# Second layer's attention: Pi spread by turns, its sums by one product with ones, the share moved from Wout to the weighted rows

## The chip, the cores and the metric

The kernel runs on one core of one Trainium2 chip. The metric is the device time of one execution in microseconds (us). Three runs of the kernel before gave 338.89, 339.13 and 342.37 us; the median is 339.13 us. Engines: PE is TensorE, DVE is VectorE, ACT is ScalarE, POOL is GpSimd, SP issues most DMAs. Each has its own instruction stream; they meet only through semaphores.

## The reference, cut to what matters

Two layers act on x of shape (16, 256, 128); each adds attention times silu(feed-forward) to x. The first layer is a softmax attention beside a mixture of experts; the change leaves it alone. The attention of the second layer (16 heads of 8 numbers, one softmax over the heads for each row):

```python
w = (x @ Wqkv.T).reshape(b, n, h, d).transpose(0, 2, 1, 3)
w_normed = w / jnp.maximum(norm, EPS_NORM)
logits = jnp.sum(w_normed * w_normed, axis=-1) * temp[None, :, :]
Pi = jax.nn.softmax(logits, axis=1)
Pi_norm = Pi / (jnp.sum(Pi, axis=-1, keepdims=True) + EPS_PI)
dots = jnp.einsum('bhn,bhnd->bhd', Pi_norm, w * w)
attn = 1.0 / (1.0 + dots)
out = -(w * Pi[..., None]) * attn[:, :, None, :]
return out.reshape(b, n, dim) @ Wout.T + bout
```

`attn` is one number for each column of a batch element. It can be put on the weighted rows or on Wout's rows. The feed-forward of the second layer picks one of 8 experts for each batch element, from its last row, and loads that expert's weights: they can be fetched only once the choice is known.

## The kernel before, in words

Everything stays in SBUF as 32 tiles of 128 rows. A batch element b is two tiles, a chunk c is two batch elements (b = 2c and 2c+1), so there are 16 elements and 8 chunks. All sums are kept transposed in the second layer: the 128 partitions are the columns of w (16 heads of 8), the free axis is the row n.

For a chunk the second layer goes: `norm1` (DVE, layer norm), `turn1` (PE, four transposes, copied out by ACT), `proj` (PE, w), `squares` (ACT, w squared with its norm) and `keep` (ACT, w itself into FT), `weigh` (DVE, the weights of the heads), `heads` (PE, logits, 16 columns), `center` (DVE), `soft` (ACT), `share` (DVE: Pi), `expand` (ACT: each of the 16 shares copied 8 times along the free axis, so that a tile of 128 rows holds 128 numbers each). Then for each b:

- `spread(b, k)` (PE, L664 to L671): two f32 products of the expanded Pi with identity and a column of ones (129 columns) into bank PS[k]. The first 128 columns are Pi turned, the last one its sum over the rows.
- `dots(b, k)` (DVE, L1316 to L1321): one custom instruction multiplies and adds up Pi times w squared (L1319, with an accumulator read behind it); one reduction adds the two sums (L1321).
- `attn_out(b, k)` (DVE, L1323 to L1326): w times Pi, into FT. It is the last reader of bank k and raises `s_ot`.

For a chunk `attention(c)` (DVE, L1328 to L1338) is three small dependent steps that give the share ATT, `weigh_out(c)` (ACT, L1757) makes two copies of Wout scaled by it, and `out1(c, k)` (PE, L673) multiplies the rows of FT by them. `end(c, k)` (DVE, L1344) adds the result to x, and SP stores it.

The feed-forward shares the engines: `ff_up` (L690), `ff_down` (L698), `ff_out` (L713) on PE, with gelu and bias on ACT and the residual on DVE (L1342). `choose1`, `choose2` (PE), `sel_logits`, `select` (DVE) choose the experts of eight elements at once (g = 0, 1); `select(1)` releases SP's loads of the experts 8 to 15 (L285 to L287).

The order of work on each engine is written out by hand: one list of calls for each engine. The eight PSUM banks are handed out by hand too. The third argument on PE names the semaphore to wait for before a bank is overwritten: `out1(1, 5, s_ot, 5)` waits until five `attn_out` are done, that is `attn_out(4, 5)`, and `heads(5, 2, s_ot, 7)` until `attn_out(6, 2)` is. Work behind such a wait on PE waits too.

Of the kernel before, what the change touches and what calls it, by code (L numbers as in the profile page):

```python
# [11 lines left out]
ALU = mybir.AluOpType  # L12
# [62 lines left out]
def program(nc, D, out):  # L75
    with ExitStack() as ctx:
# [3 lines left out]
        def sem(name):  # L80
# [71 lines left out]
        WOB = EP[:, 1, :].rearrange("p (b d) -> p b d", d=128)  # L152
# [33 lines left out]
        s_selx, s_soft, s_px, s_wob, s_h1, s_rt, s_g1 = (sem(n) for n in (  # L186
            "sel_exp", "soft", "pi_spread", "wout_weighted", "h1", "reasoned", "end_silu"))
# [138 lines left out]
        def _(e):  # L326
# [337 lines left out]
            def spread(b, k, free=None, n=0):  # L664
# [4 lines left out]
                for i in range(2):  # L669
                    m = e.matmul(PS[k][:, i * 129:(i + 1) * 129], PXP[c % 2][:, h, i * 128:(i + 1) * 128], C[:, 0:129], start=True, stop=True)  # L670
                m.then_inc(p_sp, 1)  # L671

            def out1(c, k, free=None, n=0):  # L673
                e.wait_ge(s_wob, c + 1)
# [5 lines left out]
                for i in range(4):  # L680
                    m = e.matmul(PS[k][:, i * 128:(i + 1) * 128], tile(WT, 4 * c + i), WOB[:, (2 * c + i // 2) % 8, :],
                                 start=False, stop=i == 3)
# [224 lines left out]
        def _(e):  # L907
# [405 lines left out]
            def pi(k):  # L1313
                return PS[k][:, 0:258].rearrange("p (i n) -> p i n", i=2)

            def dots(b, k):  # L1316
                e.wait_ge(p_sp, b + 1)
                w2 = w2v(b).rearrange("p (i n) -> p i n", i=2)
                e.tensor_tensor_reduce(w2, pi(k)[:, :, 0:128], w2, 1.0, 0.0, ALU.mult, ALU.add,  # L1319
                                       DOT[:, b:b + 1]).then_inc(s_vec, v.up())  # L1320
                e.tensor_reduce(SPI[:, b:b + 1], pi(k)[:, :, 128], AX, ALU.add).then_inc(s_vec, v.up())  # L1321

            def attn_out(b, k):  # L1323
                w = tile(WT, 2 * b, 2).rearrange("p (i n) -> p i n", i=2)
                e.wait_ge(s_w, b // 2 + 1)
                e.tensor_tensor(w, pi(k)[:, :, 0:128], w, ALU.mult).then_inc(s_ot, 1)  # L1326

            def attention(c):  # L1328
# [9 lines left out]
                                       op1=ALU.mult).then_inc(s_attn, 1)  # L1338

# [100 lines left out]
            attn_out(0, 6)  # L1440
            weigh(2)
            dots(1, 0)
            center(2, 4)
# [4 lines left out]
            attention(0)  # L1448
            attn_out(2, 5)
            dots(3, 2)  # L1450
            sel_logits(0, 7)
            attn_out(3, 2)
            attention(1)
# [14 lines left out]
            attn_out(4, 5)  # L1468
# [17 lines left out]
            attention(3)  # L1486
# [9 lines left out]
            dots(9, 3)  # L1496
            attn_out(8, 7)
# [4 lines left out]
            dots(11, 7)  # L1502
# [570 lines left out]
```

## Time and profile before

| | before |
|---|---|
| median of three runs | 339.13 us |
| lowest, highest run | 338.89, 342.37 us |
| span of the profiled execution (first to last instruction) | 338.1 us |
| granted TensorE clock, mean over the span | 0.995 of full |
| PE busy | 312.5 us (92%) |
| DVE busy | 208.9 us (62%) |
| ACT busy | 206.7 us (61%) |
| POOL busy | 138.5 us (41%) |

The profiled execution's own device time is not listed beside its span. The shortest run, 338.89 us, is 0.8 us above the span, the median 1.0 us. The second layer's attention, the part that changes, lies between 249 us (the first `spread`) and the end. The chain of waits names, for each moment, the work that the end of the program hung on. The timeline lists instructions of one engine by start; where an engine sat idle before, the row tells how long and what released it. A busy engine's rows overlap a little, so the cost of a step is best read as the distance between the starts of neighbours.

### The profile page before, as it was taken

The page shows a single profiled execution, that of the slowest core. Times are in us where ns is not written, and L with a number is a line of the kernel's source. Part 1 is how long each engine was busy: PE and PEld are TensorE (multiplying, and loading weights), DVE is VectorE, ACT ScalarE, POOL GpSimd, SP SyncE. Part 2 cuts the span into 40 slices and gives each one's busy share as a digit, 9 for nine tenths or more (in the row PEclk, how much of TensorE's full clock was granted, in tenths as well). Part 3 has the DMA queues.
Part 4 walks back from the last instruction along what each step waited for, and adds up shares of the span by engine and source line. Part 5 has one row for each costly group of instructions (what it writes and reads, how often), then busy time and mean ns, then how long its engine had stood idle before and what let it go on. Part 6 is the DMA issues. An engine that isn't in the chain of part 4 may idle for free.

```text
span 338.1 us, 7770 instructions
## 1 busy us (share of the span) xinstructions
PE 312.5 (92%) x2077; PEld 259.6 (77%) x2077; DVE 208.9 (62%) x779; ACT 206.7 (61%) x504; POOL 138.5 (41%) x152
## 2 busy tenths in 40 slices
PE   7879999999999799999998899898879999989994
PEld 6657555669999799999988767688854588768793
DVE  4999792225776765556544457665365848578465
ACT  2296754348776666565654435674586768897772
POOL 2200577777777746666664434454540000000000
PEclk9999999999999999999999999999997999999999
DMA  6980023113431113333333721111006532017403
GB/s 187 294 367 4 32 66 104 56 49 87 105 95 57 48 33 89 94 92 87 103 94 108 261 65 35 55 33 33 31 7 244 120 77 57 3 32 211 133 17 109
DMA packets 29321, 31.91 MB, mean 94 GB/s; under 512 B 7120, under 2 KB 22610, under 8 KB 29152
## 3 DMA queue, kind: packets, MB, share of 16 engines
q1 hardware_dynamic: 24960, 22.97, 24.1%
q0 software_dynamic: 4320, 8.47, 7.5%
q8 instruction: 18, 0.29, 0.4%
q14 instruction: 23, 0.19, 0.2%
HBM read 19.86 MB, written 12.01 MB: 94 GB/s over the span
## 4 chain that ended last, share of the span: by engine, by line
PE 72%; DVE 11%; ACT 5%; issue 5%; SPq 2%; DMA 2%; DVEq 1%; ACTq 0%
PE PS L474 19%; PE PS L486 9%; PE PS L414 4%; PE PS L690 3%; PE PS L401 3%; PE PS L440 3%; PE PS L698 3%; PE PS L626 2%; PE PS L390 2%; PE PS L392 2%; PE PS L627 2%; PE PS L642 2%; PE PS L628 2%; DVE XA L924 2%; PE PS L454 2%
## 5 line engine op out<-in xcount | busy, mean ns | idle before, releaser
L2010 POOL DMA_INDIRECT yc_scratch<-YS,XS x71 | 71.6, 1009 | 61.1 <-ACT YS L1609 44.6
L474 PE MATMUL PS<-XG,XT 128*128 128x128 f32 x568 | 76.7, 278 | 6.9 <-issue 3.0
L474 PEld LDWEIGHTS PS<-XG,XT 128*128 128x128 f32 x568 | 69.0, 192 | 10.1 <-issue 6.3
L1126 DVE COPY XT<-WE 128x512 f32 x71 | 30.9, 435 | 38.5 <-issue 21.3
L1602 ACT ACTIVATE EP<-PS 128x256 f32<-128x256 f32 x71 | 27.0, 383 | 43.3 <-PE PS L474 42.3
L486 PE MATMUL PS<-WE,EP 128*128 x284 | 43.9, 278 | 1.9 <-ACT YS L1609 1.8
L2001 POOL DMA_INDIRECT xs_scratch<-XA,POS x32 | 31.4, 981 | 29.9 <-DVE POS L1035 20.5
L486 PEld LDWEIGHTS PS<-WE,EP 128*128 128x128 f32 x284 | 37.6, 191 | 5.9 <-issue 5.9
L1117 DVE TENSOR_TENSOR EP<-EP,PS 128x256 f32<-128x256 f32 x71 | 29.6, 417 | 18.4 <-PE PS L486 15.9
L2001 POOL DMA_INDIRECT xs_scratch<-XB,POS x32 | 31.2, 976 | 9.8 <-issue 9.8
L1609 ACT ACTIVATE YS<-PS,XS 128x128 f32<-128x128 f32 x71 | 26.0, 366 | 5.2 <-PE PS L486 2.0
L944 DVE TENSOR_TENSOR EP<-EP,PS 128x512 f32<-128x512 f32 x16 | 10.8, 684 | 17.4 <-PE PS L392 17.4
L924 DVE TENSOR_SCALAR XA<-X,MV,RS 128x128 f32<-128x128 f32 x64 | 18.8, 362 | 0.6
L1578 ACT ACTIVATE EP<-EP,NM 128x256 f32<-128x256 f32 x32 | 15.9, 500 | 4.0 <-PE PS L428 4.0
L440 PE MATMUL PS<-F,EP 128*128 128x128 f32 x128 | 16.3, 276 | 1.7 <-DVE EP L1109 1.7
L401 PEld LDWEIGHTS PS<-WB,EP 128*128 128x128 f32 x128 | 15.1, 192 | 3.3 <-DVE EP L944 2.3
L440 PEld LDWEIGHTS PS<-F,EP 128*128 128x128 f32 x128 | 15.5, 192 | 2.1 <-DVE EP L1109 1.9
L913 DVE BATCH_NORM_STATS2 ST<-X 128x6 f32<-128x128 f32 x64 | 13.7, 276 | 4.8 <-DMA X<-in_x 4.8
L1093 DVE CUSTOM_DVE_ANT_0 EP<-PS,C 128x256 f32<-128x256 f32 x32 | 12.3, 420 | 6.9 <-PE PS L414 4.2
L390 PE MATMUL PS<-XT,WB 128*128 128x512 f32 x32 | 16.5, 597 | 0.0
L401 PE MATMUL PS<-WB,EP 128*128 128x128 f32 x128 | 15.9, 277 | 0.6 <-DVE EP L944 0.6
L392 PE MATMUL PS<-XT,WB 128*128 128x512 f32 x32 | 16.3, 592 | 0.0
(190 smaller groups left out, 601.3 us busy)
## 6 DMA issues: line engine op xcount, KB each, us to landing
XS<-xs_scratch SPq DMA_DIRECT2D x71, 65.0 KB, 1.9
XB<-yc_scratch SPq DMA_DIRECT2D x16, 256.0 KB, 4.4
S<-in_w SPq DMA_DIRECT2D x13, 256.0 KB, 2.6
WE<-in_we SPq DMA_DIRECT2D x1, 3072.0 KB, 14.8
X<-in_x SPq DMA_DIRECT2D x16, 128.0 KB, 3.0
out<-X SPq DMA_DIRECT2D x16, 128.0 KB, 1.8
yc_scratch<-YS,XS POOLq DMA_INDIRECT x71, 2.3
SH<-in_w SPq DMA_DIRECT2D x3, 256.0 KB, 2.5
```

Of the source, the lines that this page charges most:

```text
L390: e.matmul(PS[k][:, :], WB[:, f * 128:(f + 1) * 128], tile(XT, 4 * c, 4), start=True, stop=True).then_inc(p_g, 1)
L401: m = e.matmul(PS[1][:, t * 128:(t + 1) * 128], HHS[:, (2 * c + f) % 3, t * 128:(t + 1) * 128], WB[:, 512 + f * 128:512 + (f + 1) * 128], ...
L440: m = e.matmul(PS[k][:, i * 128:(i + 1) * 128], PT[:, kb, j, i * 128:(i + 1) * 128], F[:, 2 * b + j, :], start=j == 0, stop=j == 1)
L474: m = e.matmul(PS[k][:, f * 128:(f + 1) * 128], WC[:, u % 4, f * 128:(f + 1) * 128], XG[:, g % 2, j * 128:(j + 1) * 128], start=True, stop ...
L486: m = e.matmul(PS[k][:, 0:128], HHE[:, u % 3, f * 128:(f + 1) * 128], WE[:, bass.ds(reg[u] + (512 + f * 128), 128)], start=f == 0, stop=f ...
L924: m = e.tensor_scalar(XA[:, t, 0:128], X[:, t, :], MV[:, t, 0:1], RS[:, t:t + 1], ALU.subtract, ALU.mult)
L1117: e.tensor_tensor(HHE[:, u % 3, :], SGE[:, u % 3, :], PS[u % 3 if u < BESIDE else u % 2][:, 256:512], ALU.mult).then_inc(s_hhe, 1)
L1126: e.tensor_copy(WC[:, u % 4, :], WE[:, bass.ds(r, 512)]).then_inc(s_wc, 1)
L1602: e.activation(SGE[:, u % 3, :], PS[u % 3 if u < BESIDE else u % 2][:, 0:256], ACT.Silu, bias=0.0, scale=1.0).then_inc(s_sge, 1)
L1609: e.activation(YS[:, u % 8, :], PS[(5, 7)[u % 2] if u < BESIDE else 5][:, 0:128], ACT.Copy, bias=0.0, scale=XS[:, g % 4, j, 129:130]).then ...
L2001: e.indirect_dma_start(out=xs, out_offset=bass.IndirectOffsetOnAxis(ap=POS[:, s, t:t + 1], axis=0), in_=T[:, t, :], in_offset=None, bounds ...
L2010: e.indirect_dma_start(out=yc, out_offset=bass.IndirectOffsetOnAxis(ap=XS[:, g % 4, j, 128:129].bitcast(U32), axis=0), in_=YS[:, u % 8, :] ...
```

## The change: Pi turned instead of multiplied, sums for a chunk at once, the share on the rows

1. `spread` transposes the expanded Pi (two transposes for each b). For the first element of a chunk it adds one product of ones (128x128) with the chunk's 64 columns of Pi: 64 sums, one for each tile and head, in every partition, in columns 256 to 319 of the same bank.
2. `sums(c, k)` on DVE takes each element's 32 columns, masks them with the head of the partition and adds them up: two custom instructions for a chunk, the second after a wait for the first (they share a scratch). The reduction in `dots` goes.
3. `attn_out` multiplies by Pi and by the share ATT in one instruction, and so waits for `attention(c)`. `weigh_out` on ACT goes with its buffer and semaphore, and `out1` multiplies by Wout itself as soon as both `attn_out` of its chunk are done.
4. The list of DVE is reordered: `dots(2c)`, `dots(2c+1)`, `attention(c)`, and only then the two `attn_out`. The list of PE has the same calls in the same order with the same bank guards.

```diff
 def spread(b, k, free=None, n=0):
                 for i in range(2):
-                    m = e.matmul(PS[k][:, i * 129:(i + 1) * 129], PXP[c % 2][:, h, i * 128:(i + 1) * 128], C[:, 0:129], start=True, stop=True)
+                    m = e.transpose(PS[k][:, i * 128:(i + 1) * 128], PXP[c % 2][:, h, i * 128:(i + 1) * 128], ident)
+                if h == 0:
+                    m = e.matmul(PS[k][:, 256:320], ONE[:, 0:128], LG[:, c, :, :].rearrange("p i h -> p (i h)"),
+                                 start=True, stop=True)
 def out1(c, k, free=None, n=0):
-                e.wait_ge(s_wob, c + 1)
+                e.wait_ge(s_ot, 2 * c + 2)
...
+            def sums(c, k):
+                sc = WA[:, 84:116].rearrange("p (i h) -> p i h", i=2)
+                for h in range(2):
+                    if h == 1:
+                        e.wait_ge(s_vec, v.n)
+                    e.tensor_tensor_reduce(sc, PS[k][:, 256 + 32 * h:288 + 32 * h].rearrange("p (i h) -> p i h", i=2),
+                                           c_("head").unsqueeze(1).broadcast_to([128, 2, 16]), 1.0, 0.0, ALU.mult, ALU.add,
+                                           SPI[:, 2 * c + h:2 * c + h + 1]).then_inc(s_vec, v.up())
 def dots(b, k):
-                e.tensor_reduce(SPI[:, b:b + 1], pi(k)[:, :, 128], AX, ALU.add).then_inc(s_vec, v.up())
+                if b % 2 == 0:
+                    sums(b // 2, k)
 def attn_out(b, k):
-                e.tensor_tensor(w, pi(k)[:, :, 0:128], w, ALU.mult).then_inc(s_ot, 1)
+                e.wait_ge(s_attn, b // 2 + 1)
+                e.scalar_tensor_tensor(out=w, in0=pi(k), scalar=ATT[:, b:b + 1], in1=w, op0=ALU.mult,
+                                       op1=ALU.mult).then_inc(s_ot, 1)
...
 # DVE's list, chunks 2 and 3
             dots(4, 5)
             norm1(4)
-            attn_out(4, 5)
             norm1(5)
             ff_out(1, 7)
             norm1(6)
             dots(5, 2)
+            attention(2)
+            attn_out(4, 5)
             norm1(7)
             weigh(4)
             attn_out(5, 2)
-            attention(2)
             center(4, 3)
             dots(6, 2)
             weigh(5)
+            dots(7, 6)
+            attention(3)
             attn_out(6, 2)
-            dots(7, 6)
             center(5, 2)
...
 # ACT: weigh_out(0) to weigh_out(7) taken out of the list
```

**First place, DVE around `attn_out(4)`.** Before, from `dots(4)` (L1319) over `norm1(4)` to `attn_out(4)` (L1326, which frees bank 5):

```order
L1319 ISA F,SM<-PS5,F 128x256 [waits pe_spread]
L1319 ISA SM 128x1
L1321 TENSOR_REDUCE SM<-PS5 128x1
L921 RECIPROCAL RS<-RS 128x4 [waits deviation1]
L924 TENSOR_SCALAR XA<-X,MV,RS 128x128 [waits vector_steps]
L924 TENSOR_SCALAR XA<-X,MV,RS 128x128 x3
L1326 TENSOR_TENSOR FT<-PS5,FT 128x256 [waits w_kept]
```

Now the end of `norm1(5)`, then `ff_out(1)` (L1356), `norm1(6)`, `dots(5)` (L1333), `attention(2)` and `attn_out(4)` (L1351):

```order
L926 TENSOR_SCALAR XA<-X,MV,RS 128x128 x3
L1356 SCALAR_TENSOR_TENSOR F<-PS7,XA 128x512 [waits pe_ff_out]
L923 RECIPROCAL RS<-RS 128x4 [waits deviation1]
L926 TENSOR_SCALAR XA<-X,MV,RS 128x128 [waits vector_steps]
L926 TENSOR_SCALAR XA<-X,MV,RS 128x128 x3
L1333 ISA F,SM<-PS2,F 128x256 [waits pe_spread]
L1333 ISA SM 128x1
L1339 SCALAR_TENSOR_TENSOR SM<-SM 128x2 [waits vector_steps]
L1342 RECIPROCAL SM<-SM 128x2 [waits vector_steps]
L1344 SCALAR_TENSOR_TENSOR SM<-SM 128x2 [waits vector_steps]
L1351 SCALAR_TENSOR_TENSOR FT<-PS5,SM,FT 128x256 [waits attention,w_kept]
```

`attn_out(4)` has moved behind two layer norms, one `ff_out`, `dots(5)` and `attention(2)`. On PE the step that overwrites bank 5 (`out1(1)`, after `turn1(4)`) stands where it stood.

**Second place, DVE around `attn_out(6)`, which frees bank 2.** Before, from `dots(6)` to `dots(7)` (bank 6), with `weigh(5)` (L1271 to L1277) between:

```order
L1319 ISA F,SM<-PS2,F 128x256 [waits pe_spread]
L1319 ISA SM 128x1
L1321 TENSOR_REDUCE SM<-PS2 128x1
L1271 TENSOR_SCALAR SM<-SM 128x2 [waits norm2]
L1273 RECIPROCAL SM<-SM 128x2 [waits vector_steps]
L1277 TENSOR_TENSOR WB<-SM 128x32 [waits vector_steps]
L1326 TENSOR_TENSOR FT<-PS2,FT 128x256 [waits w_kept]
L1319 ISA F,SM<-PS6,F 128x256 [waits pe_spread]
```

Now, from the end of `sums(3)` on:

```order
L1324 ISA SM 128x1
L1333 ISA F,SM<-PS2,F 128x256
L1333 ISA SM 128x1
L1273 TENSOR_SCALAR SM<-SM 128x2 [waits norm2]
L1275 RECIPROCAL SM<-SM 128x2 [waits vector_steps]
L1279 TENSOR_TENSOR WB<-SM 128x32 [waits vector_steps]
L1333 ISA F,SM<-PS6,F 128x256 [waits pe_spread]
L1333 ISA SM 128x1
L1339 SCALAR_TENSOR_TENSOR SM<-SM 128x2 [waits vector_steps]
L1342 RECIPROCAL SM<-SM 128x2 [waits vector_steps]
```

`dots(7)` and `attention(3)` now stand before `attn_out(6)`, which is the next row but one.

**Third place, PE from `spread(6)` to `heads(5)`, the step that overwrites bank 2.** Before:

```order
L670 MATMUL PS2<-C,SH 128x129 [waits attn_out,pi_spread]
L670 MATMUL PS2<-C,SH 128x129
L634 MATMUL PS4<-C,XA 128x128 [waits xt1,xn]
L634 MATMUL PS4<-C,XA 128x128 x3
L642 MATMUL PS3<-XT,WD 128x512 [waits centered,xt1]
L670 MATMUL PS6<-C,SH 128x129 [waits w_kept,pi_spread]
L670 MATMUL PS6<-C,SH 128x129
L649 MATMUL PS2<-WB,F 128x16 [waits attn_out,head_weights]
```

Now:

```order
L669 MATMUL PS2<-C,SH 128x128 [waits attn_out,pi_spread]
L669 MATMUL PS2<-C,SH 128x128
L671 MATMUL PS2<-C,ONE 128x64
L633 MATMUL PS4<-C,XA 128x128 [waits xt1,xn]
L633 MATMUL PS4<-C,XA 128x128 x3
L641 MATMUL PS3<-XT,WD 128x512 [waits centered,xt1]
L669 MATMUL PS6<-C,SH 128x128 [waits w_kept,pi_spread]
L669 MATMUL PS6<-C,SH 128x128
L648 MATMUL PS2<-WB,F 128x16 [waits attn_out,head_weights]
```

Nothing moved here: `heads(5)` still follows `spread(7)` directly and still waits for `attn_out(6)`; only what it waits for has moved on DVE.

## Rows read from the trace of the kernel before

**Rows 1.** The page: the chain that ended last, share of the span by engine.
```profile
PE 72%; DVE 11%; ACT 5%; issue 5%; SPq 2%; DMA 2%; DVEq 1%; ACTq 0%
```
**Rows 2.** Chain of waits in order of time, 255 to 301 us: start us, us, what.
```profile
300.75 0.24 DVE SELI L1303 x2
```
**Rows 3.** Single lines of code: duration ns min/median/max, first and last start us.
```profile
L670 PE MATMUL PS<-C,EP x32: 273/275/356, 250.6 to 316.7; 128*128 128x129 f32 x32
...
L634 PE MATMUL PS<-C,XA x32: 272/273/332, 216.5 to 292.2; 128*128 128x128 f32 x32
...
L1762 ACT ACTIVATE EP<-WD,SM x16: 384/392/401, 257.1 to 327.9; 128x128 f32<-128x128 f32 x16
```
**Rows 4.** PE timeline, 282 to 305 us: start, us, what, idle before.
```profile
282.51 0.61 PE L713 MATMUL PS<-WD,WB 128*128 128x128 f32 x4
...
283.82 0.60 PE L634 MATMUL PS<-C,XA 128*128 128x128 f32 x4
284.26 0.38 PE L618 MATMUL PS<-BR,ROWS 128*128 128x512 bf16 x1
...
291.36 0.69 PE L670 MATMUL PS<-C,SH 128*128 128x129 f32 x4
...
293.19 0.61 PE L670 MATMUL PS<-C,SH 128*128 128x129 f32 x4
293.63 0.98 PE L649 MATMUL PS<-WB,F 128*128 128x16 f32 x8
294.46 0.37 PE L656 MATMUL PS<-XT,WD 128*128 128x8 f32 x2
...
304.76 1.13 PE L690 MATMUL PS<-XT,S 128*128 128x256 f32 x4 [1.67 <-DMA WA<-in_b]
```
**Rows 5.** DVE timeline, 279 to 286 us.
```profile
280.46 0.18 DVE L921 RECIPROCAL RS<-RS 128x4 f32<-128x4 f32 x1 [0.84 <-ACT RS L1534]
...
283.28 0.68 DVE L1342 SCALAR_TENSOR_TENSOR F<-PS,XA 128x512 f32<-128x512 f32 x1
283.88 0.16 DVE L921 RECIPROCAL RS<-RS 128x4 f32<-128x4 f32 x1
...
285.11 0.42 DVE L1319 CUSTOM_DVE_ANT_0 F<-PS,F 128x256 f32<-128x256 f32 x1
285.45 0.08 DVE L1319 DVE_READ_ACCUMULATOR2_ANT SM<- 128x1 f32 x1
```
**Rows 6.** DVE timeline, 289 to 294 us: `attention(2)`, then `dots(7)`.
```profile
289.24 0.15 DVE L1332 SCALAR_TENSOR_TENSOR SM<-SM 128x2 f32<-128x2 f32 x1
289.42 0.17 DVE L1335 RECIPROCAL SM<-SM 128x2 f32<-128x2 f32 x1
289.62 0.16 DVE L1337 SCALAR_TENSOR_TENSOR SM<-SM 128x2 f32<-128x2 f32 x1
...
293.83 0.42 DVE L1319 CUSTOM_DVE_ANT_0 F<-PS,F 128x256 f32<-128x256 f32 x1 [0.40 <-PE PS L670]
```
**Rows 7.** Groups of DVE work, 249 to 338 us: busy us, mean ns of one.
```profile
L1285 DVE TENSOR_TENSOR C<-PS,WA 128x64 f32<-128x64 f32 x6 | 1.3, 224 | 0.2
L1277 DVE TENSOR_TENSOR WB<-SM 128x32 f32<-128x32 f32 x6 | 1.1, 192 | 0.2
```
**Rows 8.** Stretches: length, busy PE, PEld, DVE, ACT, POOL, granted clock, DMA, GB/s.
```profile
246.90:249.60 2.70, 1.58 (x12) 1.35 (x12) 1.99 (x9) 2.67 (x6) 1.73 (x2) 1.00 0.05 9
...
256.00:259.40 3.40, 3.40 (x6) 1.44 (x6) 1.59 (x9) 2.39 (x5) 0.00 (x0) 0.50 0.95 347
...
301.00:304.70 3.70, 2.03 (x15) 1.65 (x15) 3.18 (x17) 3.08 (x7) 0.00 (x0) 1.00 0.42 82
```
**Rows 9.** Chain of waits: the same `add_up` steps on PE at either clock.
```profile
256.12 1.88 PE PS L626 x2
258.00 1.63 PE PS L627 x2
...
261.67 0.86 PE PS L627 x2
```

More of the change, by code:

```diff
@@ L1318, in dots @@
                 w2 = w2v(b).rearrange("p (i n) -> p i n", i=2)
[L1319 to L1326 removed]
+                if b % 2 == 0:
+                    sums(b // 2, k)
+                e.tensor_tensor_reduce(w2, pi(k), w2, 1.0, 0.0, ALU.mult, ALU.add, DOT[:, b:b + 1]).then_inc(s_vec, v.up())
             def attention(c):
@@ L1338, in attention, with attn_out @@
                                        op1=ALU.mult).then_inc(s_attn, 1)
+            def attn_out(b, k):
+                w = tile(WT, 2 * b, 2).rearrange("p (i n) -> p i n", i=2)
+                e.wait_ge(s_w, b // 2 + 1)
+                e.wait_ge(s_attn, b // 2 + 1)
+                e.scalar_tensor_tensor(out=w, in0=pi(k), scalar=ATT[:, b:b + 1], in1=w, op0=ALU.mult,
+                                       op1=ALU.mult).then_inc(s_ot, 1)
             def ff_out(c, k):
@@ L1439, in _ @@
             dots(0, 6)
-            attn_out(0, 6)
             weigh(2)
             dots(1, 0)
+            attention(0)
+            attn_out(0, 6)
             center(2, 4)
@@ L1447, in _ @@
             center(3, 6)
-            attention(0)
+            dots(3, 2)
+            attention(1)
             attn_out(2, 5)
-            dots(3, 2)
             sel_logits(0, 7)
             attn_out(3, 2)
-            attention(1)
             select(0)
@@ L1485, in _ @@
             attn_out(7, 6)
-            attention(3)
             center(6, 4)
@@ L1496, in _ @@
             dots(9, 3)
+            attention(4)
             attn_out(8, 7)
@@ L1502, in _ @@
             dots(11, 7)
+            attention(5)
             end(2, 4)
@@ L1509, in _ @@
             dots(12, 6)
-            attention(4)
             dots(13, 0)
+            attention(6)
             ff_out(4, 5)
             attn_out(12, 6)
-            attention(5)
             attn_out(13, 0)
-            attention(6)
             dots(14, 3)
+            dots(15, 1)
+            attention(7)
             attn_out(14, 3)
-            dots(15, 1)
             attn_out(15, 1)
             ff_out(5, 7)
-            attention(7)
             end(4, 2)
@@ L1755, in expand @@
                 m.then_inc(s_px, 1)
-            def weigh_out(c):
-                e.wait_ge(s_attn, c + 1)
-                if c >= 4:
-                    e.wait_ge(p_o1, c - 3)
-                for b in (2 * c, 2 * c + 1):
-                    m = e.activation(WOB[:, b % 8, :], d_("wout"), ACT.Copy, bias=0.0, scale=ATT[:, b:b + 1])
-                m.then_inc(s_wob, 1)
             def ff_up(b, k):
@@ L1889, in _ @@
             choose1(0, 1)
-            weigh_out(0)
             soft(2)
@@ L1893, in _ @@
             soft(3)
-            weigh_out(1)
             gated(4, 4)
@@ L1924, in _ @@
             squares(5, 6)
-            weigh_out(2)
             keep(5, 6)
@@ L1938, in _ @@
             keep(7, 2)
-            weigh_out(3)
             expand(5)
@@ L1967, in _ @@
             gate1(5)
-            weigh_out(7)
             ff_down(14, 0)
```

12 lines of the change are left out of this document (4 added, 8 removed).

## The prediction, written before the changed kernel ran

> **What bounds the kernel now.** I read the page's chain first: PE carries 72% of it, DVE 11%, DMA and SP's queue 2% each [rows 1]. So work taken off PE should count, and a wait put on PE should count in full, except where PE itself waits for somebody. The chain in order of time shows where it does in the changed part: from 256 to 295 us it is PE's own work almost without a break, then it turns to DVE (`center(6)` to `select(1)`, the choice of the second eight experts, done at 300.99 [rows 2]), to SP, and to the load of an expert's weights; PE stood still for 1.67 us and took up `ff_up(8)` at 304.76 [rows 4]. `select(1)` hangs on `choose1`, `choose2` and `heads(6)`, which stand on PE behind `heads(5)`. So whatever delays PE before 297 us delays the load and all that follows. The end of the program is PE-bound again, with a short tail on DVE and one store. The kernel is tight in this sense: a saving on PE is worth itself, and the guards of the banks decide whether there is a saving at all.
>
> **PE's work.** A f32 product leaves two records here: 16 `spread` of two products would be 64, half of them reading EP are 32 [rows 3]. A transposed tile leaves one: 8 `turn1` of four tiles are 32 [rows 3]. The distance from start to start is 0.44 us for four records of either kind: 283.82 to 284.26 for four transposes, 293.19 to 293.63 for the two products of `spread(7)` [rows 4]. So two transposes take 0.22 where two products took 0.44: minus 0.22 us for each of 16 elements, 3.5 us. The product with ones, two passes of 64 columns, is not in the trace. Its bounds are passes of 16 columns, 0.83 us for eight (293.63 to 294.46 [rows 4]), 0.10 each, and passes of 129 columns, 0.11 each; I take 0.21 for two. Eight of them add 1.7 us. The first `spread` of a chunk thus changes by 0.01, the second by 0.22. Where PE carries the chain that is: `spread(5)` at 270 us, `spread(11)` at 308 and `spread(15)` at 324; `spread(1)` and `(3)` lie before a wait of PE for DVE, `(9)` and `(13)` before waits for weights, and `(7)` is dealt with below.
>
> **ACT's work.** `weigh_out` goes, 16 instructions of 0.39 us, 6.3 us in all [rows 3]. ACT waits for PE or DVE before nearly every group in this part, so I cost the gain at nothing; nothing in the places below waits for ACT. `out1` needed the scaled Wout before and needs the two `attn_out` now; it stands so late in PE's list that neither is what it waits for, with one exception, next but one.
>
> **DVE's work.** Each chunk gets two masked sums over 32 columns. Their nearest rows are a tensor operation on 32 columns, 0.19 us, and one reading 64 columns of PSUM, 0.22 [rows 7], each with an accumulator read that costs about 0.01 beyond overlap (285.11 and 0.42 against 285.45 and 0.08 [rows 5]) and a wait of some 0.04 between them: 0.46 for the pair, with 0.40 and 0.60 as bounds. The reduction saved two times 0.07. `attn_out` with a scalar I cost like before, 0.42: on 512 columns the three-operand form took 0.68 (283.28 [rows 5]), less than twice 0.42. Eight chunks give 8 x (0.46 - 0.14), about 2.5 us more on DVE, which has idle time nearly everywhere. What counts is not this work but the order.
>
> **First new stall: `out1(1)` on PE waits for `attn_out(4)`.** Before, PE began it at 284.26 [rows 4], two us after DVE had freed bank 5. PE is 0.22 early by then (`spread(5)`), so it will ask at 284.04. DVE: `norm1(4)` waited 0.84 us for ACT's root and began at 280.46 [rows 5]; that idle time swallows the sums of chunk 2, and the root comes with PE, so it begins at 280.24. `norm1(4)` and `norm1(5)` take 1.23 each (the distance 283.88 to 285.11 [rows 5]), `attn_out(4)` no longer stands between them, and they end at 282.70. `ff_out(1)` waits for PE's product, 282.51 + 0.61 - 0.22 [rows 4], so it starts at 282.92, and takes 0.60 (283.28 to 283.88 [rows 5]). `norm1(6)` takes 1.23 again, to 284.75. `dots(5)` to the end of its accumulator read takes 0.42 (285.11 to 285.53 [rows 5]): 285.17. `attention(2)` starts 0.04 later and takes 0.54 (289.24 to 289.78 [rows 6]): 285.75. Another 0.04 for its own semaphore, then `attn_out(4)` 0.42: 286.21. With 0.04 to PE, `out1(1)` starts at 286.25. That is 1.99 us later than before, and 2.21 us of idle PE. Behind it stand `ff_down(5)`, `proj(4)` and everything up to the choice of experts, none of which had slack on PE: all moves by 1.99.
>
> **Second new stall: `heads(5)` waits for `attn_out(6)`.** `spread(7)` starts at 293.19 + 1.99 = 295.18. Its second transpose ends 0.11 + 0.27 later, 295.56, and `dots(7)` follows in 0.03 as before (293.19 + 0.61 to 293.83 [rows 4, 6]). DVE is there in time: `spread(6)` ends at 291.36 + 0.69 + 1.99 = 294.04 [rows 4], then `sums(3)` 0.46, `dots(6)` 0.42 and the three small steps of `weigh(5)`, 0.52 (like the first three of `attention`), come out at 295.5 with 0.1 to spare; this is the one place where dearer sums would show. Then 0.42 for `dots(7)`, 0.04 + 0.54 for `attention(3)`, 0.04 + 0.42 for `attn_out(6)`, 0.04 to PE: 295.59 + 1.50 = 297.09. Before, `heads(5)` began at 293.63 [rows 4]: it is 3.46 late, 1.47 more than the first stall left. `center(5)` to `select(1)`, SP and the load have nothing of their own that was waited for in parallel, so `ff_up(8)` starts at 304.76 + 3.46 = 308.22.
>
> **After that** the other moved `attn_out` are late by 0.7 to 1 us on DVE, but their banks are asked for later still: `spread(11)` wants `attn_out(8)` 4 us after it was done, `out1(3)` wants `attn_out(9)` 3 us after, the others 1.5 us or more. `end(2)` comes about 0.6 later against the rest and its store just keeps its turn in SP's queue before the load of expert 13; at most 0.3 could come of it. `spread(11)` and `spread(15)` give back 0.22 each.
>
> **Sum:** + 1.99 + 1.47 - 0.44, and 0.02 for the first `spread`s of later chunks: + 3.0 us on a span of 338.1, 341.1. The median of the runs stands 1.03 above that span, so the time is 339.13 + 3.0 = **342.2 us**, 0.9% slower. I call anything within 1%, 335.7 to 342.5 us, no change, since that is about what a measurement of this kernel can tell.
>
> **A rule against the change.** The clock fell once in the changed part: 0.50 (the 1.2 GHz level) from 256.0 to 259.4 [rows 8], and that cost (1.88 - 0.86) + (1.63 - 0.86) = 1.8 us [rows 9]. In 246.9 to 249.6, where 8 transposes were 1.04 of PE's 1.58 busy us, it stayed at 1.00 [rows 8]. The Trainium skill (TensorE: Matmul & The Clock Gate, Part 4: PE-mode transpose) says that transposes do not count as busy for the clock gate as products do. By that rule the clock would drop where transposes replace products next to idle time; the rows of this case neither bear it out nor exclude it.
>
> **Rivals.**
> - *The clock falls once more* (chance 0.22). Two new waits of 2.2 and 1.5 us, and shorter `spread`s around the wait for weights, leave PE less to do between 284 and 308 us. For: the fall at 256.0 shows that this part can lose the clock. Against: from 301 to 304.7 PE was busy only 2.03 of 3.7 us and kept it [rows 8]. Price as in [rows 9]: up to 1.8 us on the path, 342.2 + 1.8 = 344.0, or 343.3 if only part of it meets chained work.
> - *The guards don't bind and only the savings stay* (0.06): the other side. PE would gain 3 to 4 times 0.22, 338.3 us. It decides at one point: `attn_out(4)` done before 284.04 and `attn_out(6)` before 295.4. For it speaks that DVE is 62% busy; against it that the five steps in front of `attn_out(4)` all have their durations in the rows and 2.2 us would have to go.
> - *Only the first stall costs* (0.12): some of what follows `heads(5)` was late for a reason that I don't see, and swallows the second. 342.2 - 1.5 = 340.7 us.
> - *The turn isn't cheaper* (0.05): if a transpose fed by the expanded Pi needed two passes, nothing is saved on PE and each product with ones adds 0.21, six of them on the path: + 0.66 + 1.2, 344.0 us. The one record for each tile in [rows 3] speaks against it.
>
> The forecast keeps 0.55, with 341.6 to 342.9 as its own range (sums at 0.60 add 0.05 to 0.2, waits of DVE at 0.06 instead of 0.04 add 0.1, the store 0.3); about a third of it lies above 342.5. Slower by over 1%: 0.55/3 + 0.22 + 0.05 = 0.45; within 1%: 0.37 + 0.12 + 0.04 = 0.53; faster by over 1%: 0.02, part of the second rival. The range 340.5 to 344.2 leaves out the second rival, the upper edge of the first and half of the fourth.
>
> **What would show it.** `out1(1)` on PE with 2.2 us idle before it, released by DVE's `attn_out`; `heads(5)` with 1.5 us idle before it; two records for each `spread` and two more for each chunk; `weigh_out` gone from ACT with no new wait on ACT; `ff_up(8)` near 308.2. I am wrong if PE has no wait at `out1(1)`, if a step of `attention` with its waits takes more than 0.25, or if the clock's row shows a second fall.

## The result: 2.4% slower, outside the range

Beside runs of the kernel before on the same chip, the changed kernel took 349.5 us in the median of 4 runs (347.72 to 354.24), the kernel before 340.75 us (338.89 to 345.58). The ratio is 1.0236, with a 95% interval of 1.015 to 1.0322. Another 6 runs, in a later set, gave 350.42 against 340.86 us, 1.0237 [1.0186, 1.0288]. Every ratio here is taken over the executions that are not more than 1.5% above the fastest of their kernel, while the medians and means of times count all of them. The forecast was 342.2 us (340.5 to 344.2). So 8 to 10 us were lost (8.0 and 8.1 by the ratios, 8.8 and 9.6 by the medians) where 3.0 were forecast.

The profiled execution of the changed kernel was the longest of the four: 354.24 us, span 352.4 us, mean granted clock 0.944 (0.952 to 0.975 in the other three). What it shows of the clock's falls is therefore more than usual. The page has the chain by engine, which answers to [rows 1], and the clock in 40 slices of 8.8 us:

```profile
PE 79%; DVE 9%; issue 4%; ACT 3%; DMA 2%; SPq 1%; DVEq 1%; ACTq 0%
PEclk9678999999999999999999999999789998858998
```

PE's share of the chain grew from 72 to 79%, though the change took work off PE. The second row shows one reason: the clock is down in three places. Slices 2 to 4 lie in the first layer, which the change leaves alone; slices 29 and 30 hold a longer form of the fall that before had too [rows 8]; slices 34 to 37 are new. The last slice holds a fall from 350.2 us on, at the end of the program.

The PE timeline around the two places of the prediction, 289 to 336 us (start, us, what, idle before):

```profile
289.08 0.60 PE L633 MATMUL PS<-C,XA 128*128 128x128 f32 x4
292.01 0.42 PE L617 MATMUL PS<-BR,ROWS 128*128 128x512 bf16 x1 [2.34 <-DVE FT L1351]
292.23 1.92 PE L683 MATMUL PS<-WD,FT 128*128 128x128 f32 x8
...
302.53 0.38 PE L669 MATMUL PS<-C,SH 128*128 128x128 f32 x2
304.71 1.04 PE L648 MATMUL PS<-WB,F 128*128 128x16 f32 x8 [1.81 <-DVE FT L1351]
305.60 0.37 PE L655 MATMUL PS<-XT,WD 128*128 128x8 f32 x2
306.42 0.20 PE L661 MATMUL PS<-WD,A 128*8 128x8 f32 x2 [0.45 <-ACT A L1750]
306.54 2.08 PE L641 MATMUL PS<-XT,WD 128*128 128x512 f32 x2
...
318.11 1.81 PE L692 MATMUL PS<-XT,S 128*128 128x256 f32 x4
```

Both forecast stalls are there with the releaser forecast: `out1(1)` (the row at 292.01) waited 2.34 us for `attn_out`, `heads(5)` (304.71) 1.81 us. They answer to the rows of 284.26 and 293.63 in [rows 4], which had no wait. Behind each stands something that wasn't forecast: eight products of L683 took 1.92 us, where eight of the same kind took 1.05 later (323.20), and `proj` (L641) 2.08 where it took 1.02 at 299.10. And `ff_up(8)` (318.11) no longer waits for its weights at all, as it did in [rows 4]: PE itself had become later than the load. The stretches give the clock (columns as in [rows 8]):

```profile
249.00:258.00 9.00, 7.19 (x29) 5.34 (x29) 4.43 (x19) 6.24 (x15) 3.98 (x5) 0.63 0.04 10
292.00:295.40 3.40, 3.38 (x13) 3.10 (x14) 1.10 (x4) 0.00 (x0) 0.00 (x0) 0.53 0.00 0
306.60:320.00 13.40, 13.40 (x53) 11.35 (x53) 7.27 (x38) 9.17 (x24) 0.00 (x0) 0.52 0.19 46
```

The clock was at its lower level (0.50 of full, 1.2 GHz) for 3.4 us right behind the first stall (292.2 to 295.6) and for 13.6 us behind the second (305.9 to 319.5), of which PE was busy for all of the 3.4 and for 13.2 of the 13.6 us: it was the bound there. Behind the second stall come narrow products, `heads` of 16 columns and the choices of 8.

DVE before `out1(1)`, to be held against [rows 5] and [rows 6], and the pair of sums:

```profile
284.40 0.16 DVE L1324 CUSTOM_DVE_ANT_1 WA<-PS,C 128x32 f32<-128x32 f32 x1
284.49 0.08 DVE L1324 DVE_READ_ACCUMULATOR2_ANT SM<- 128x1 f32 x1
284.61 0.19 DVE L1324 CUSTOM_DVE_ANT_1 WA<-PS,C 128x32 f32<-128x32 f32 x1
284.72 0.08 DVE L1324 DVE_READ_ACCUMULATOR2_ANT SM<- 128x1 f32 x1
...
290.71 0.16 DVE L1339 SCALAR_TENSOR_TENSOR SM<-SM 128x2 f32<-128x2 f32 x1
290.91 0.17 DVE L1342 RECIPROCAL SM<-SM 128x2 f32<-128x2 f32 x1
291.11 0.16 DVE L1344 SCALAR_TENSOR_TENSOR SM<-SM 128x2 f32<-128x2 f32 x1
291.38 0.48 DVE L1351 SCALAR_TENSOR_TENSOR FT<-PS,SM,FT 128x256 f32<-128x256 f32 x1
```

### The profile page after: what moved, and what is told of

The parts are those of the page before. It is cut to its first block, busy times and chain, and to the rows that moved or that the text cites. A ratio compares the mean times of both kernels' runs of the same rounds, so it can differ in the third digit from the quotient of the medians.

```text
span 352.4 us, 7750 instructions
## 1 busy us (share of the span) xinstructions
PE 324.6 (92%) x2061; PEld 269.2 (76%) x2061; DVE 212.4 (60%) x795; ACT 202.8 (58%) x488; POOL 138.5 (39%) x152
## 4 chain that ended last, share of the span: by engine, by line
PE 79%; DVE 9%; issue 4%; ACT 3%; DMA 2%; SPq 1%; DVEq 1%; ACTq 0%
PE PS L473 18%; PE PS L485 9%; PE PS L692 4%; PE PS L413 4%; PE PS L700 4%; PE PS L439 4%; PE PS L400 4%; PE PS L389 3%; PE PS L391 3%; PE PS L641 2%; PE PS L715 2%; PE PS L347 2%; PE PS L625 2%; PE PS L683 2%; PE PS L627 2%
## 5 line engine op out<-in xcount | busy, mean ns | idle before, releaser
L485 PE MATMUL PS<-WE,EP 128*128 x284 | 45.0, 283 | 2.3 <-ACT YS L1623 1.8
L485 PEld LDWEIGHTS PS<-WE,EP 128*128 128x128 f32 x284 | 38.5, 195 | 6.4 <-issue 6.2
L400 PEld LDWEIGHTS PS<-WB,EP 128*128 128x128 f32 x128 | 16.4, 206 | 3.2 <-DVE EP L946 2.5
L389 PE MATMUL PS<-XT,WB 128*128 128x512 f32 x32 | 18.3, 656 | 0.0
L400 PE MATMUL PS<-WB,EP 128*128 128x128 f32 x128 | 17.2, 292 | 0.6 <-DVE EP L946 0.6
L391 PE MATMUL PS<-XT,WB 128*128 128x512 f32 x32 | 17.5, 628 | 0.0
L1776 ACT ACTIVATE SH<-PS,WA 128x256 f32<-128x256 f32 x32 | 13.2, 473 | 6.7 <-PE PS L692 3.4
```

What stands on the lines that cost most here:

```text
L389: e.matmul(PS[k][:, :], WB[:, f * 128:(f + 1) * 128], tile(XT, 4 * c, 4), start=True, stop=True).then_inc(p_g, 1)
L391: e.matmul(PS[k + 1][:, :], WB[:, 256 + f * 128:256 + (f + 1) * 128], tile(XT, 4 * c, 4), start=True, stop=True).then_inc(p_u, 1)
L400: m = e.matmul(PS[1][:, t * 128:(t + 1) * 128], HHS[:, (2 * c + f) % 3, t * 128:(t + 1) * 128], WB[:, 512 + f * 128:512 + (f + 1) * 128], ...
L485: m = e.matmul(PS[k][:, 0:128], HHE[:, u % 3, f * 128:(f + 1) * 128], WE[:, bass.ds(reg[u] + (512 + f * 128), 128)], start=f == 0, stop=f ...
```

## How the runs are compared

Every run lists its span and mean granted clock. I call (1 - clock) x span its **lost clock**: 19.7 us in the profiled execution after, 1.7 before. Of the 19.7 us, 8.5 lie in the two falls behind the stalls (half of 3.4 and of 13.6) and 6.9 in the unchanged first layer (half of 10.3 and of 3.4). Over 143 runs on the chips of the second and third group, runs of one kernel differ by 0.63 us of time for each us of lost clock (worked out by a line with one slope and one height for each kernel, with a standard error of 0.02; one execution of 1122.70 us, told of below, is left out). With that, a difference of mean times splits into one at equal clock and one that the clock made. For the changed kernel against before on the chip of the second group: 351.4 - 341.2 = 10.2 us, of which 0.63 x (14.9 - 4.9) = 6.3 are clock and 3.9 are not. The split is an estimate, good to about 1 us: over the 115 of these runs that the ratios count the slope is 0.44 (0.04), and of 9.1 us, at 13.3 against 4.0 us of lost clock, 4.1 are clock and 5.0 are not.

Places in different traces, and the falls of the clock, are given from the start of the second layer's first `ff_up`. By that measure (us): `out1(1)`, `heads(5)` and `ff_up(8)` stood at 15.88, 25.25, 36.38 before, and at 18.15, 30.85, 44.25 after; the forecast was 17.87, 28.71, 39.84.

Two theories went in. One (G): the two stalls cost what was forecast, and the clock falls behind them, because a stall leaves PE with little to do. The other (T): transposes take clock away by being transposes, wherever they replace products.

## First group: one part of the change at a time

On this chip every kernel, before too, took some 85 us longer, in the unchanged first layer (before: median 426.56 us of 23 runs, lost clock 42.2). Only differences are used.

**Turns alone.** The kernel before, with its order of work, its `attn_out` and `weigh_out`; only `spread`, the product with ones and the sums are changed, with a wait for DVE's own work ahead of both sums.

```diff
-                    m = e.matmul(PS[k][:, i * 129:(i + 1) * 129], PXP[c % 2][:, h, i * 128:(i + 1) * 128], C[:, 0:129], start=True, stop=True)
+                    m = e.transpose(PS[k][:, i * 128:(i + 1) * 128], PXP[c % 2][:, h, i * 128:(i + 1) * 128], ident)
+                if h == 0:
+                    m = e.matmul(PS[k][:, 256:320], ONE[:, 0:128], ...)
```

> Parts 1 and 2 alone: Pi is turned and summed by ones, but the share stays on Wout and the order of DVE is the old one (one more wait of DVE for itself ahead of each pair of sums). Theory G (late bank guards make PE idle, and the clock falls behind the idle time): no wait of PE at out1(1) or heads(5), full clock from 260 us on, 338 to 340 us where the kernel before has 339 to 341, that is -1 to 0 us. Theory T (transposes in place of products lose the clock by themselves): the granted clock is low somewhere between 284 and 320 us and the time is 342 us or more.

Measured: 428.79 us, 1.0036 [0.9996, 1.0076], lost clock 46.1. Neither of the two stalls, `ff_up(8)` at 36.45. In its profile the clock fell once in the changed part before the end, from 35.4 to 42.2 us behind the first `ff_up`, that is where PE waits for the weights of expert 8. So turning Pi saves nothing that can be measured, and the lost clock is some 4 us above that of before.

The trace also shows a small new wait at `heads(5)`, where the kernel before has none [rows 4]. `attn_out(6)` on DVE before, then `attn_out(6)` and `heads(5)` here:

```profile
293.01 0.42 DVE L1326 TENSOR_TENSOR FT<-PS,FT 128x256 f32<-128x256 f32 x1
```

```profile
383.68 0.42 DVE L1338 TENSOR_TENSOR FT<-PS,FT 128x256 f32<-128x256 f32 x1
384.24 1.04 PE L649 MATMUL PS<-WB,F 128*128 128x16 f32 x8 [0.47 <-DVE FT L1338]
```

`spread(7)` started 0.29 us earlier than before (24.52 against 24.81) and `heads(5)` 0.12 later (25.37 against 25.25): the sums of chunk 3 stand on DVE ahead of `dots(6)` and `attn_out(6)`, for which `heads(5)` waits. From the end of `attn_out(6)` to the start of `heads(5)` it is 0.14 us here and was 0.20 before: that guard had opened only just before PE asked, so what PE saved up to here turned into waiting.

**Rows alone.** The changed kernel's order of work, `attn_out` with the share and no `weigh_out`, but Pi spread by products as before.

```diff
-                    m = e.transpose(PS[k][:, i * 128:(i + 1) * 128], ...)
+                    m = e.matmul(PS[k][:, i * 129:(i + 1) * 129], ..., C[:, 0:129], start=True, stop=True)
```

> Parts 3 and 4 alone: products of 129 columns as before, the share on the rows, the new order of DVE. Theory G: PE is idle for 2.0 us or so before out1(1) and 1.5 before heads(5), the clock falls behind at least one of them, and the time is close to the changed kernel's, +6 to +10 us over before. Theory T: the two stalls alone, +3.5 us, and the clock stays at 1.00 after them.

Measured: 434.42 us, 1.0196 [1.0138, 1.0254], lost clock 48.4. The PE timeline at the two places:

```profile
370.36 0.59 PE L617 MATMUL PS<-BR,ROWS 128*128 128x512 bf16 x1 [2.41 <-DVE FT L1338]
...
383.25 1.47 PE L648 MATMUL PS<-WB,F 128*128 128x16 f32 x8 [1.88 <-DVE FT L1338]
```

The same stalls, with no turned Pi in the kernel, and the clock fell behind both: 18.1 to 21.5 and 31.8 to 42.0 us on the common scale, where the changed kernel had 18.4 to 21.8 and 32.0 to 45.7. This tells the theories apart for most of the loss: it doesn't need the transposes (1.0196 here, 1.0237 for the whole change). It comes with the order of work.

**One stall.** The kernel before, with only `attn_out(4)` moved.

```diff
-            attn_out(4, 5)
...
             dots(5, 2)
+            attention(2)
+            attn_out(4, 5)
```

> The kernel before with nothing changed but one place in DVE's order: attn_out(4) stands behind norm1(5), ff_out(1), norm1(6), dots(5) and attention(2). Theory G: out1(1) waits 1.5 to 2 us; +1.5 to +2 us if the clock holds, +3 to +4 if it falls to 0.50 for about 3.4 us right after. Theory T: +2 us at most, clock untouched.

Measured: 430.44 us, 1.0038 [0.9997, 1.0079], lost clock 42.6; `out1(1)` waited 2.15 us and the clock fell once, from 18.1 to 21.5. In its profile `ff_up(8)` is at 40.00, 3.6 us late for a stall of 2.15: the clock takes the rest. But its runs lost hardly more clock than those of before, and of the 3.6 us only 1.6 are in the time by the ratio, with an interval from 0 to 3.4 (2.7 by the means of all runs: 429.99 against 427.28). That this stall alone costs clock in most executions isn't shown.

**The stalls filled.** The changed kernel with products in both stalls whose results nobody reads: 18 ahead of `out1(1)`, 13 ahead of `heads(5)`, 256 columns each, into banks that are free.

```diff
+            def fill(k, free, n, times):
+                e.wait_ge(free, n)
+                for _ in range(times):
+                    e.matmul(PS[k][:, 0:256], BFC[:, 1, 0:128], BFC[:, 1, :], start=True, stop=True)
+            fill(0, s_h1, 6, 18)
             out1(1, 5, s_ot, 5)
+            fill(4, s_xt1, 8, 13)
             heads(5, 2, s_ot, 7)
```

> The changed kernel with products of ones (bf16, 256 columns) whose results nobody reads put before the two guards: 18 before out1(1), 13 before heads(5), into banks that PE has to wait for next anyway. They end before the guards open or within 0.3 us. Theory G: the two waits last as long as before or shrink to what the filling leaves, but the clock stays at 1.00 behind them; the time falls by 3 to 6 us against the changed kernel, to 343 to 346. Theory T: the clock falls as in the changed kernel, time as there or a little above.

Measured: 431.65 us, 1.0115 [1.0057, 1.0172], lost clock 45.8: by the medians 2.8 us less than rows alone, which has the same stalls open; the two intervals overlap. The stalls are there still, as filled time, and behind the first one the clock stayed up:

```profile
368.00:372.00 4.00, 3.65 (x30) 3.08 (x29) 3.62 (x15) 3.30 (x6) 0.00 (x0) 1.00 0.00 0
372.00:381.00 9.00, 9.00 (x55) 6.98 (x54) 3.55 (x20) 5.54 (x16) 0.00 (x0) 1.00 0.00 1
```

Behind the second it fell later than before and for less long (32.0 to 38.8), so there the filling didn't keep it, against theory G. `heads(5)` stood at 29.20, 1.65 us earlier than in the changed kernel, without a single wait taken away.

## Second group: the second stall, and ways out

Before: 340.86 us (29 runs), lost clock 4.7 (median), 4.9 (mean).

**The changed kernel again**, unchanged.

> The changed kernel itself, beside the others of this set. Measured from the start of ff_up(0): out1(1) at 18.2 us with 2.3 us of idle PE before it, heads(5) behind 1.8 us of idle PE, and the clock low for one stretch behind the first wait and for two or more behind the second. If the falls belong to the kernel and not to the one execution that was profiled, they come again; if they were chance, the end is at 74 to 75 us from ff_up(0) instead of 78.5. Time +7 to +10 us over before.

Measured: 350.42 us, 1.0237 [1.0186, 1.0288], lost clock 15.3. The first result comes again, and so do the stalls (2.33 and 1.81 us) with a fall behind each (18.4 to 21.9 and 32.1 to 35.5). A third fall came at 42.3 to 49.2. `ff_up(8)` stood at 43.26, this time behind a wait of 1.62 us for its weights. This profiled execution lost 18.3 us of clock, again more than the mean of 14.9.

**The other stall alone.** The kernel before, with only `attn_out(6)` moved.

```diff
-            attn_out(6, 2)
             dots(7, 6)
+            attention(3)
+            attn_out(6, 2)
...
-            attention(3)
```

> The kernel before with one other place of DVE's order changed: attn_out(6) stands behind dots(7) and attention(3). heads(5) then waits about 1.5 us. Theory G with equal waits: +1.5 us, and +1.7 more if the clock falls for one stretch, +3.4 to +5 if it stays low for two or three stretches as behind this wait in the changed kernel. If only the sum of both waits makes the clock stay low, it falls once at most here.

Measured: 344.11 us, 1.0097 [1.0064, 1.013], lost clock 6.7. The PE timeline:

```profile
295.79 1.04 PE L649 MATMUL PS<-WB,F 128*128 128x16 f32 x8 [1.61 <-DVE FT L1326]
```

A stall of 1.61 us costs 3.3 us; in the profile the clock fell once behind it (28.4 to 31.9), and in the runs 2.2 us of the 3.3 stay at equal clock. By the ratios the two stalls alone cost 1.6 and 3.3 us, 4.9 together, and the changed kernel 8.1; by the means of all runs it is 2.7 and 3.4, 6.1 together, and 10.2. The stalls alone lost 0.4 and 1.9 us of clock, the changed kernel 10.6 (medians against before). So the two stalls in one kernel cost more than one by one. The turns aren't needed for that: rows alone, with both stalls and no turned Pi, costs 8.4 us by the ratio. Why two stalls cost more than their sum isn't shown.

**The order mended.** The changed kernel with `attn_out(4)` early again behind an earlier `attention(2)`, and `proj(6)` and `choose1(1)` on PE put between `spread(7)` and `heads(5)`.

```diff
             dots(4, 5)
+            dots(5, 2)
+            attention(2)
+            attn_out(4, 5)
             norm1(4)
...
-            proj(6, 3, s_ctr, 5)
             spread(7, 6, s_w, 6)
-            heads(5, 2, s_ot, 7)
+            proj(6, 3, s_ctr, 5)
             choose1(1, 4, s_xt1, 8)
+            heads(5, 2, s_ot, 7)
```

> The changed kernel with the guards met earlier. DVE: dots(5), attention(2) and attn_out(4) stand right behind dots(4), ahead of the layer norms. PE: spread(7) before proj(6), choose1(1) before heads(5). No wait at out1(1), 0.3 to 0.9 us at heads(5). Theory G: the clock keeps 1.00 behind out1(1), falls at most once after 30 us; time within 1% of before, -1 to +3 us, and 5 us or more under the changed kernel. Theory T: still +5 us or more over before.

Measured: 344.29 us, 1.0088 [1.0055, 1.0122], lost clock 9.9. `out1(1)` came at 15.66 without a wait. `heads(5)` still waited, for 1.34 us where 0.3 to 0.9 were expected, even with both ahead of it, and the clock fell from 29.1 to 35.9:

```profile
302.30 1.04 PE L648 MATMUL PS<-WB,F 128*128 128x16 f32 x8 [1.34 <-DVE FT L1351]
```

At equal clock it is 0.2 us from before (338.3 against 338.1), 3.7 less than the changed kernel (342.0). What is left, 0.63 x (10.4 - 4.9) = 3.5 us, is clock. (Over the runs that the ratios count it is 1.1 us from before at equal clock.)

**Turns with a filling.** Turns alone, with 14 unread products ahead of `ff_up(8)`, where turns alone had lost the clock.

```diff
+            fill(2, s_w, 8, 14)
             ff_up(8, 2, s_w, 8)
```

> The kernel with turns and sums alone (share on Wout, old order of DVE), whose profile showed the clock low around the wait for weights before ff_up(8), and 14 products of ones that nobody reads put into that wait (bf16, 256 columns, 1.5 us). Theory G: what matters is how much PE does, so the clock keeps 1.00 there and the time is 1 to 2 us under the kernel with turns alone, at or under before. Theory T: no better than turns alone.

Measured: 342.66 us, 1.0023 [0.998, 1.0065], lost clock 7.5. The clock no longer fell at this place, and `ff_up(8)` waited 0.17 us instead of 1.67; it started no later (36.46). But its profile lost clock further back (53.8 to 57.3) and before the changed part. The loss was not tied to this one place. `heads(5)` waited 0.47 us here too.

## Third group: transposes against the clock

Before: 339.89 us (29 runs), lost clock 3.7.

**Turned twice.** Turns alone, with each transpose issued two times, the second into the same columns.

```diff
-                for i in range(2):
+                for i in (0, 1, 0, 1):
                     m = e.transpose(PS[k][:, i * 128:(i + 1) * 128], ...)
```

> Turns and sums alone (share on Wout, old order of DVE), with every transpose of the spread issued twice into the same place: PE has as many records there as with products. Theory G in the form that what counts is how much PE does: the span lost to the low clock (one minus the mean granted clock, times the span, median of the runs) comes back to that of before, near 4.7 us, and the time is 1 to 2 us over before for the products with ones. Theory T: it stays at the 8 to 9 us that turns alone lose, and the time is 3 to 4 us over before.

Measured: 342.08 us, 1.0024 [0.9986, 1.0062], lost clock 4.7. One of its 12 executions took 1122.70 us at a granted clock of 1.00; it has no profile, its cause is open, and the lost clock is that of the other 11. The saving is gone by construction (64 records in place of the 64 of the products), and with it most of the additional lost clock; at equal clock it is 1.4 us above before (339.0 against 337.6), as much as eight products with ones at 0.17. The stretch from the end of the first layer over the whole middle of the part that changes:

```profile
246.90:310.00 63.10, 57.87 (x327) 44.19 (x327) 43.95 (x211) 50.62 (x124) 3.97 (x5) 1.00 0.29 82
```

The clock is at 1.00 over 63 us, with 64 transposes of Pi in the kernel beside the 32 of `turn1`. (In this profile it is at 1.00 all the way from 19.5 to 336.9 us.) `heads(5)` has no wait here (0.07 us). This speaks against T: in this execution PE kept the clock with transposes in the time that products filled, and over the runs turned twice lost 0.9 us more clock than before (means, standard error 0.9). It isn't decided by it: against turns with five fillings, further down on the same chip, the difference is 2.3 us with a standard error of 1.3. That what costs clock is that PE has less to do fits all of this, but it is argued.

**The changed kernel filled.** Fillings at both stalls and at five more places at which PE waits: 8 and 4 ahead of the second to last and last experts of the first layer, 4 ahead of `heads(3)`, 10 ahead of `ff_up(8)`, 6 ahead of `ff_up(14)`.

```diff
+            fill(6, s_xg, 18, 8)
             down_e(69)
+            fill(6, s_xg, 18, 4)
             down_e(70)
+            fill(6, s_ot, 1, 4)
             heads(3, 6, s_ot, 1)
+            fill(0, s_h1, 6, 18)
             out1(1, 5, s_ot, 5)
+            fill(4, s_xt1, 8, 13)
             heads(5, 2, s_ot, 7)
+            fill(2, s_w, 8, 10)
             ff_up(8, 2, s_w, 8)
+            fill(4, s_h1, 13, 6)
             ff_up(14, 4, s_h1, 13)
```

> The changed kernel with products of ones that nobody reads in six of PE's waits: before out1(1) (18) and heads(5) (13) as in the earlier filled kernel, and before down_e(69) (8), down_e(70) (4), heads(3) (4), ff_up(8) (10) and ff_up(14) (6). Theory G: the span lost to the clock falls from 15 to 8 us or less, and the time from +9.6 to +3 to +5 us over before: what remains are the waits. Theory T: less than 2 us better than the changed kernel.

Measured: 344.66 us, 1.014 [1.0089, 1.0191], lost clock 6.3 where the changed kernel had 15.3. Set against the before of its own chip each time, the changed kernel is 8.1 us slower by the ratio and this one 4.8 (by the medians 9.6 and 4.8): 3 to 5 us come back from work that nobody needs. The same stretch, and the PE timeline at the second stall:

```profile
246.90:310.00 63.10, 59.48 (x340) 44.48 (x341) 43.38 (x208) 45.36 (x111) 2.91 (x3) 1.00 0.27 79
```

```profile
294.50 0.38 PE L674 MATMUL PS<-C,SH 128*128 128x128 f32 x2
294.72 1.58 PE L632 MATMUL PS<-BFC 128*128 128x256 bf16 x13
296.69 1.04 PE L653 MATMUL PS<-WB,F 128*128 128x16 f32 x8 [0.39 <-DVE FT L1363]
```

The clock is full here from 221.6 us until PE has ended, so this trace shows the forecast itself, since the fillings end before or as the guards open: `out1(1)` at 18.17 (forecast 17.87), `heads(5)` at 29.21 (forecast 28.71), `ff_up(8)` at 40.13 (39.84), the end 72.92 us behind the first `ff_up`, 3.2 later than before (69.72), where the sum said 3.0.

**The kernel before filled.** The five additional fillings, not those at the stalls, put into the kernel before.

> The kernel before with the same products of ones in the five waits that it has itself: before down_e(69), down_e(70), heads(3), ff_up(8), ff_up(14). Theory G: the fall near 256 us goes or gets rarer, lost span 2 to 4 instead of 4.7 us, time -0.5 to -2 us. Theory T says nothing on it; if the filling is in the way, +0.5 us.

Measured: 339.15 us, 0.9966 [0.9934, 0.9999], lost clock 2.5. It has the lowest median of all kernels run; the interval ends so close below 1 that it is faster only by a hair, if at all. Its profile has no fall between 19.1 and 336.5 us. The changed kernel filled, on the same chip, is 5.5 us above it (medians).

**Turns, filled at five places.** The same five in turns alone.

> Turns and sums alone with the same five fillings. At equal clock the turns were 2.0 us faster than before; with the clock held by the fillings this is the version that could beat both: -1 to -3 us against before. If turns lose the clock whatever stands in the waits (theory T), it stays at 0 to +1 us.

Measured: 341.42 us, 1.0014 [0.9985, 1.0043], lost clock 7.8. Its profiled execution was an odd one (375.73 us, mean clock 0.835, at 0.85 over most of the span) and says nothing on the others. The 2.0 us that the expectation starts from isn't borne out: with the slope of 0.63, turns alone in the first group are 0.8 us faster at equal clock. Here, at equal clock, it is within 0.1 us of before (337.7 against 337.6). The nearest comparison is the kernel before with the same fillings: leaving out the odd execution, this one takes 2.7 us more (means, standard error 1.0) and loses 3.8 us more of clock (1.2). So turns lost more clock than products in spite of the fillings, which is what T says; that PE has less to do with one transpose for each product says it too.

## Why the prediction was wrong, step by step

- **First stall: right, 0.3 us too small.** `out1(1)` came 2.27 us late where 1.99 were forecast. In the rows of DVE: `attention(2)` to the start of `attn_out` took 0.67 (290.71 to 291.38), not 0.58; `attn_out` with the share 0.48, not 0.42; from its end to PE's start 0.15, not 0.04.
- **Second stall: right, 0.3 us too small** for the same three reasons: 2.18 us from `spread(7)` to `heads(5)`, against 1.91.
- **PE's work: right in kind.** Two records for a `spread`, two for the ones. A first `spread` of a chunk takes 0.39 us from start to start (274.72 to 275.11), so the product with ones costs 0.17, not 0.21.
- **The sums: 0.32 for the pair** (284.40 to 284.72), not 0.46, and they delayed nothing. `weigh_out` on ACT could go for nothing, as forecast: no wait for ACT took its place on PE at the two stalls.
- **The sum: right at equal clock, somewhat small.** +3.0 forecast; +3.9 from the runs (up to 5.0, by which runs give the slope), +3.2 from the filled kernel's trace.
- **The step that failed is the clock, put at nothing in the sum and at too little in the first rival's price**, "up to 1.8 us on the path" for "the clock falls once more". The rival was given a chance of 0.22 and the size of one fall as before had it [rows 9]. In the profile it fell once behind the first stall and for four times as long behind the second, 17.0 us in all at half speed, with PE busy for 16.6 of them; over the runs the kernel lost 10.0 us more of clock than before (means), worth 6.3 us. `ff_up(8)`, forecast at 39.84, was found at 44.25 in one profile and at 43.26 in the other: by there 3.4 to 4.4 us had been lost. The prediction's own signs of being wrong came too: a second fall of the clock, and a step of `attention` with its waits of 0.27 us (291.11 to 291.38), over its 0.25.
- **Why I priced it low** was the stretch 301.0 to 304.7 [rows 8], where PE was busy for 2.03 of 3.7 us and kept the clock, with a wait of 1.67 us at its end. One stretch that kept it isn't a bound. The runs show that it is a matter of chance for each execution: the changed kernel's two profiles had falls of different length behind the second stall (13.6 us in one, two falls of 3.4 and 6.8 us in the other), and between 10 and 35 us, in unchanged code, six of the nine usable profiles from the undisturbed chips lost the clock and three, before among them, kept it.
- **The rule that was weighed**, that transposes don't count for the clock gate (the Trainium skill, TensorE: Matmul & The Clock Gate, Part 4: PE-mode transpose), isn't borne out as it stands: turned twice lost 4.7 us of clock beside 3.7 of before and kept 1.00 for 63 us. That a transpose counts for less than a product isn't excluded, since the turns with five fillings lost 3.8 us more of clock than products with the same fillings. The rule alone would have led to the right sign of the clock's share, but rows alone fell without any turned Pi.
- **The savings of 0.22 on the path** can't be seen: kernels with the turns and the old order are level with before in three comparisons (alone 1.0036, with one filling 1.0023, with five 1.0014, each interval holding 1). Two things show. Up to `heads(5)` the sums on DVE held the guard of `attn_out(6)` shut until PE's saving was gone (a wait of 0.47 us in turns alone); the prediction had seen that dearer sums would show here, but not that the guard was this close without the late `attn_out`. And these kernels lost more clock: 46.1 against 42.2, 7.5 against 4.7, 7.8 against 3.7.

Left open: which share of the falls in the changed part is due to the turns and which to the stalls. Rows alone lost 6.2 us more than before on its chip, the changed kernel 10.6 on another, turns alone 3.9; these roughly add up, but they are single medians. In time, rows alone (8.4 us by the ratio) already costs what the whole change does (8.1). Whether the narrow products behind the second stall make the fall there longer was not tried on its own. And why one execution loses the clock in the first layer and another not was not tried.

## What to carry to other kernels

Price a new wait of the engine that bounds the kernel twice: by its own length, and by what follows at half clock, where the engine is busy without a break; here 4.2 us of waits (2.34 and 1.81) became 8 to 10. The longest falls came where narrow products stood behind the wait, which may be why. Taking work off PE right before a guard can be worth nothing: ask how long before PE the guard opens, and what the change puts ahead of it on the other engine. And when work is moved so that a bank is freed later, look first at who overwrites the bank: this change needed its reorder only for a scalar, and with the order mended it stood near the kernel before at equal clock (0.2 to 1.1 us), though its time stayed 0.9% above.

## What was not expected of the hardware

- Waits of PE of 1.3 to 2.4 us, with work right before and behind them, were followed by 3.4 to 13.6 us at 0.50 clock at `out1(1)` and `heads(5)`, in every profile that has such a wait there open. Not every wait of this length is followed by a fall: behind the 1.67 us ahead of `ff_up(8)` in the kernel before there was none. Unread bf16 products in the same waits, 18 and 13 of 256 columns, kept it at 1.00 behind the first wait in two profiles and behind the second in one of two; with five more fillings they brought the changed kernel 3 to 5 us nearer to before.
- The clock stayed at 1.00 over 63 us with 64 transposes of Pi, two of which took 0.22 us from start to start at 1.00 (276.03 to 276.25) and 0.43 us at 0.50 (316.73 to 317.16). Whether a transpose counts for the clock as a product does is not settled.
- DVE's multiply-and-sum on 32 columns of PSUM took 0.16 to 0.19 us with 0.08 for its accumulator read; `attn_out` with a scalar of each partition took 0.48 us on 256 columns, against 0.42 without.
- One chip held every kernel up by 85 us in code that no kernel here changes (in turns alone PE was busy for 24 of the 90 us from 45 to 135). Turns alone and rows alone were measured on it alone.
